# Second attention of a two-layer kernel: three rotating banks for transposes, another order of the steps of all engines, value products of three groups together, and the maximum subtracted in two places

## The reference, cut to what matters

```python
q = layernorm(x) @ w_q + b_q          # 128 x 256, 16 heads of 16
k = ctx @ w_k + b_k
v = ctx @ w_v + b_v
s = einsum('bhqd,bhkd->bhqk', q, k) / 4
p = softmax(s, axis=-1)
x = x + einsum('bhqk,bhkd->bhqd', p, v) @ w_o + b_o
```

## Time and profile before

| what | us |
|---|---|
| median of three runs | 687.03 (685.39 to 689.8) |
| the profiled execution, its own time | 685.72 |
| its span in the trace | 684.0 |
| busy in the span: TensorE matmuls | 545.5 |
| weight loads | 376.4 |
| VectorE | 404.1 |
| ScalarE | 296.6 |
| GpSimd | 170.5 |

### The profile page before, as it was taken

One profiled execution on the slowest core, in us unless ns is written; L12 is line 12 of the kernel. 1 busy time (PEld: TensorE's weight loads), 2 busy tenths in 40 slices (PEclk: granted clock), 3 DMA queues, 4 the chain that ended last, 5 costly groups with the idle time before them and its releaser, 6 DMA issues.

```text
span 684.0 us, 10069 instructions
## 1 busy us (share of the span) xinstructions
PE 545.5 (80%) x3430; PEld 376.4 (55%) x3430; DVE 404.1 (59%) x900; ACT 296.6 (43%) x582; POOL 170.5 (25%) x214
## 2 busy tenths in 40 slices
PE   0979998699899100996899999976149999999993
PEld 0658765344344000885676666646137777766772
DVE  6558789544499798675578887758733233211111
ACT  1436596143599695000477777752003112221210
POOL 4425441000000000002222222101035455456333
PEclk9989999799999655998699999998659999999997
DMA  8600000000000001500000000003102235554411
GB/s 266 206 0 2 1 0 2 0 0 1 0 0 0 0 0 49 197 0 1 0 2 32 2 32 2 33 1 124 35 21 97 84 120 167 176 165 134 153 54 39
DMA packets 30152, 37.57 MB, mean 55 GB/s; under 512 B 6560, under 2 KB 25888, under 8 KB 30112
## 3 DMA queue, kind: packets, MB, share of 16 engines
q1 hardware_dynamic: 27040, 29.07, 13.1%
q0 software_dynamic: 3072, 7.95, 3.8%
HBM read 30.14 MB, written 6.88 MB: 54 GB/s over the span
## 4 chain that ended last, share of the span: by engine, by line
PE 51%; DVE 18%; issue 11%; ACT 8%; DMA 6%; POOL 4%; DVEq 1%; another core or an unknown queue 0%; POOLq 0%; SPq 0%; ACTq 0%
PE pC L1390 6%; PE pA L1553 4%; DMA arena<-out,token 4%; PE pC L1427 4%; PE pB L1436 3%; PE pB L1563 3%; POOL arena L479 3%; PE pA L1421 3%; PE pB L1411 3%; PE pB L1496 2%; PE pC L1277 2%; PE pA L1351 2%; DVE arena L1011 2%; ACT arena L556 2%; PE pC L1351 2%
## 5 line engine op out<-in xcount | busy, mean ns | idle before, releaser
L453 POOL TENSOR_TENSOR arena<-KT,par 128x256 f32<-128x256 f32 x32 | 19.0, 614 | 235.2 <-PE pC L1390 210.5
L722 ACT ACTIVATE arena<-pA 128x320 f32<-128x320 f32 x64 | 27.9, 437 | 107.0 <-PE pA L1553 73.0
L1553 PE MATMUL pA<-arena 128*128 128x320 f32 x256 | 72.2, 440 | 0.9 <-ACT arena L722 0.9
L1179 DVE SCALAR_TENSOR_TENSOR arena<-pB,gcol,arena 128x256 f32<-128x256 f32 x16 | 7.1, 479 | 99.5 <-DMA arena<-out,token 96.7
L1553 PEld LDWEIGHTS pA<-arena 128*128 128x128 f32 x256 | 48.4, 192 | 23.1 <-issue 2.9
L1563 PE MATMUL pB<-arena 128*128 128x256 f32 x256 | 57.2, 381 | 3.4 <-DVE arena L1186 3.4
L1563 PEld LDWEIGHTS pB<-arena 128*128 128x128 f32 x256 | 48.1, 190 | 10.5 <-issue 4.0
L479 POOL DMA_INDIRECT arena<-token_rows,token x24 | 35.9, 1496 | 57.9 <-issue 37.4
L942 DVE TENSOR_REDUCE am<-arena (+1 forms) x48 | 32.0, 681 | 28.3 <-ACT arena L593 28.3
L1076 DVE TENSOR_REDUCE rm<-pA 128x16 f32<-128x2048 f32 x16 | 36.7, 2292 | 19.4 <-PE pA L1421 19.4
L1390 PE MATMUL pC<-wdnT,XIT 128*128 128x256 f32 x192 | 43.2, 389 | 2.4 <-DVE XIT L1031 2.4
(11 more groups left out here) (284 smaller groups left out, 1183.0 us busy)
## 6 DMA issues: line engine op xcount, KB each, us to landing
arena<-in_L_ffn_wi SPq DMA_DIRECT2D x8, 1024.0 KB, 8.5
arena<-in_L_ffn_wo SPq DMA_DIRECT2D x8, 1024.0 KB, 5.8
X<-in_x SPq DMA_DIRECT2D x4, 512.0 KB, 5.2
arena<-in_ctx SPq DMA_DIRECT2D x4, 512.0 KB, 5.8
out<-X SPq DMA_DIRECT2D x4, 512.0 KB, 2.9
token_rows<-arena SPq DMA_DIRECT2D x4, 512.0 KB, 3.0
arena<-in_L_ffn_w_up SPq DMA_DIRECT2D x1, 768.0 KB, 9.0
arena<-in_L_ffn_w_gate SPq DMA_DIRECT2D x1, 768.0 KB, 10.4
```

Of the source, the lines that this page charges most:

```text
L722: nc.scalar.activation(HT[:, u, f, :], ps[2 + f % 2][:, 0:ROWS], ACT.Relu).then_inc(s["h_relu"], 1)
L1553: last = mm(ps[2 + f % 2][:, 0:ROWS], WI[:, u, k, f * P:(f + 1) * P], XET[:, u, k, :], start=(k == 0), stop=(k == KD - 1))
```

## The change

It keeps the computation and the instructions of it, and changes where they write and in which order they stand:

- Three banks now rotate in place of two: `bank_q` and `bank_o` (the two of `pC`) and `bank_t` (`ps[4]`). `bank_q` holds c_turn, c_query and group 1; `bank_o` groups 0 and 3 and the output product; `bank_t` group 2, o_turn and a_turn.
- The groups are turned in the order 2, 0, 1, 3. The products of groups 2, 0 and 1 are one step, values_201; group 3's follow at the head of the next turn.
- The scores come at lag 0, late in the turn. less_max becomes less_first (lag 2, after add_attn) and less_last (lag 3, after attn_out and stats4). attn_out and add_attn are at lag 5, stats4 at 6, a_out at 4.
- On ScalarE exps_first is at lag 1 and late in the turn, exps_last first in the turn, and the four copies of the groups stand apart.
- The waits are those that the new order and banks need.

```diff
-        BANK_OF = (1, 1, 0, 1)
+        bank_q, bank_o, bank_t = pC[:, 0, :], pC[:, 1, :], ps[4]
+        bank_of = (bank_o, bank_q, bank_t, bank_o)
...
-            steps(act, NB, [(exps_first, 2), (os_copy, 3), (exps_last, 2), (xt_copy, 0), (pt_first, 2), (q_out, 0), (pt_second, 2), (at_copy, 3), (pt_rest, 2)])
+            steps(act, NB, [(exps_last, 2), (xt_copy, 0), (os_copy, 3), (pt_2, 2), (q_out, 0), (pt_0, 2), (exps_first, 1), (pt_1, 2), (pt_3, 2), (at_copy, 3)])
...
-            def less_max(b, u, h):
-                dve.wait_ge(s["rm_ready"], b + 1)
-                free_after(dve, s["pv_done"], b)
-                for e in range(2):
-                    part = slice(e * NH1 // 2, (e + 1) * NH1 // 2)
-                    V_.tensor_tensor(PR[:, u, part], sco[:, part], rm[:, u, part].unsqueeze(2).broadcast_to([P, NH1 // 2, P]), ALU.subtract).then_inc(s["s_sub"], 1)
-            steps(dve, NB, [(row_max, 2), (attn_out, 4), (less_max, 2), (norm3, 0), (add_attn, 4), (stats4, 5)])
+            def less_max(b, u, e):
+                part = slice(e * NH1 // 2, (e + 1) * NH1 // 2)
+                if not (isinstance(b, int) and b < 2):
+                    dve.wait_ge(s["pt_tr"], 4 * b - 5 + e)
+                V_.tensor_tensor(PR[:, u, part], sco[:, part], rm[:, u, part].unsqueeze(2).broadcast_to([P, NH1 // 2, P]), ALU.subtract).then_inc(s["s_sub"], 1)
+            def less_first(b, u, h):
+                dve.wait_ge(s["rm_ready"], b + 1)
+                less_max(b, u, 0)
+            def less_last(b, u, h):
+                less_max(b, u, 1)
+            steps(dve, NB, [(attn_out, 5), (stats4, 6), (less_last, 3), (norm3, 0), (row_max, 2), (add_attn, 5), (less_first, 2)])
...
             def c_turn(b, u, h):
                 pe.wait_ge(s["xn3"], b + 1)
-                if isinstance(b, int) and b < 4:
-                    if b >= 1:
-                        pe.wait_ge(s["qt_ready"], b)
-                else:
-                    pe.wait_ge(s["x3_ready"], b - 3)
+                if b >= 3:
+                    pe.wait_ge(s["pt_ready"], 4 * (b - 3) + 3)
+                elif b >= 1:
+                    pe.wait_ge(s["qt_ready"], b)
...
+            def turn_2(b, u, h):
+                pe.wait_ge(s["p_ready"], 2 * b + 2)
+                if b >= 2:
+                    pe.wait_ge(s["at_ready"], b - 1)
+                elif b == 1:
+                    pe.wait_ge(s["pt_ready"], 1)
+                turn_group(b, u, 2)
+            def turn_0(b, u, h):
+                pe.wait_ge(s["p_ready"], 2 * b + 1)
+                if b >= 2:
+                    pe.wait_ge(s["x3_ready"], b - 1)
+                elif b == 1:
+                    pe.wait_ge(s["pt_ready"], 4)
+                turn_group(b, u, 0)
+            def turn_1(b, u, h):
+                if b + 2 < NB:
+                    pe.wait_ge(s["qt_ready"], b + 3)
+                else:
+                    pe.wait_ge(s["pt_ready"], 4 * (b - 1) + 3)
+                turn_group(b, u, 1)
+            def turn_3(b, u, h):
+                pe.wait_ge(s["pt_ready"], 4 * b + 2)
+                turn_group(b, u, 3)
...
+            def values_201(b, u, h):
+                if b >= 1:
+                    pe.wait_ge(s["os_ready"], b)
+                value_group(b, u, 2, 1)
+                value_group(b, u, 0, 2)
+                value_group(b, u, 1, 3)
+            def values_3(b, u, h):
+                value_group(b, u, 3, 4).then_inc(s["pv_done"], 1)
             def o_turn(b, u, h):
                 pe.wait_ge(s["os_ready"], b + 1)
-                pe.wait_ge(s["pt_ready"], 4 * b + 3)
+                if b + 1 < NB:
+                    pe.wait_ge(s["pt_ready"], 4 * (b + 1) + 1)
+                else:
+                    pe.wait_ge(s["at_ready"], b)
...
             def a_turn(b, u, h):
                 pe.wait_ge(s["ao_ready"], b + 1)
-                if b + 3 >= NB:
-                    pe.wait_ge(s["x3_ready"], b)
-                else:
-                    pe.wait_ge(s["qt_ready"], b + 4)
...
             def a_out(b, u, h):
                 pe.wait_ge(s["at_ready"], b + 1)
+                if b + 1 < NB:
+                    pe.wait_ge(s["pt_ready"], 4 * (b + 1) + 4)
+                else:
+                    pe.wait_ge(s["x3_ready"], b)
...
-            flat(NB, [(scores1, 1), (o_turn, 3), (c_turn, 0), (turn_0, 2), (c_query, 0), (turn_1, 2), (values_0, 2), (a_turn, 3),
-                      (turn_2, 2), (values_1, 2), (turn_3, 2), (values_2, 2), (a_out, 3), (values_3, 2)])
+            flat(NB, [(values_3, 3), (c_turn, 0), (a_out, 4), (turn_2, 2), (c_query, 0), (turn_0, 2), (o_turn, 3), (turn_1, 2),
+                      (scores1, 0), (turn_3, 2), (a_turn, 3), (values_201, 2)])
```

More of the change, by code:

```diff
@@ L654, in xt_copy @@
                 free_after(act, s["c_q"], b)
-                nc.scalar.activation(XCT[:, u, 0:2], ps[4][:, 0:2 * P].rearrange("p (k n) -> p k n", k=2), ACT.Copy).then_inc(s["c_xt"], 1)
+                nc.scalar.activation(XCT[:, u, 0:2], bank_q[:, 0:2 * P].rearrange("p (k n) -> p k n", k=2), ACT.Copy).then_inc(s["c_xt"], 1)
             def q_out(b, u, h):
@@ L660, in q_out @@
                 for k in range(KD):
-                    last = nc.scalar.activation(QT[:, u, k, :], ps[4][:, (2 + k) * P:(3 + k) * P], ACT.Identity, scale=0.25, bias=bq[:, k:k + 1])
+                    last = nc.scalar.activation(QT[:, u, k, :], bank_q[:, (2 + k) * P:(3 + k) * P], ACT.Identity, scale=0.25, bias=bq[:, k:k + 1])
                 last.then_inc(s["qt_ready"], 1)
@@ L678, in os_copy, with pt_copy, pt_2, pt_0 @@
                 nc.scalar.activation(OS[:, u], ps[5][:, :].rearrange("p (t n) -> p t n", t=4), ACT.Copy).then_inc(s["os_ready"], 1)
[L680 to L684, removed]
+            def pt_copy(b, u, g, n):
+                act.wait_ge(s["pt_tr"], b * 4 + n)
+                nc.scalar.activation(PT[:, u, 4 * g:4 * g + 4, :], bank_of[g].rearrange("p (k n) -> p k n", k=4), ACT.Copy).then_inc(s["pt_ready"], 1)
+            def pt_2(b, u, h):
                 free_after(act, s["pv_done"], b)
[L686 to L693, removed]
+                pt_copy(b, u, 2, 1)
+            def pt_0(b, u, h):
+                pt_copy(b, u, 0, 2)
+            def pt_1(b, u, h):
+                pt_copy(b, u, 1, 3)
+            def pt_3(b, u, h):
+                pt_copy(b, u, 3, 4)
             def at_copy(b, u, h):
@@ L697, in at_copy @@
                 free_after(act, s["o_done"], b)
-                nc.scalar.activation(AT[:, u], ps[4][:, 0:2 * P].rearrange("p (k n) -> p k n", k=2), ACT.Copy).then_inc(s["at_ready"], 1)
-            steps(act, NB, [(exps_first, 2), (os_copy, 3), (exps_last, 2), (xt_copy, 0), (pt_first, 2), (q_out, 0), (pt_second, 2), (at_copy, 3), (pt_rest, 2)])
+                nc.scalar.activation(AT[:, u], bank_t[:, 0:2 * P].rearrange("p (k n) -> p k n", k=2), ACT.Copy).then_inc(s["at_ready"], 1)
+            steps(act, NB, [(exps_last, 2), (xt_copy, 0), (os_copy, 3), (pt_2, 2), (q_out, 0), (pt_0, 2), (exps_first, 1), (pt_1, 2), (pt_3, 2), (at_copy, 3)])
             rsqrt(4, NB)
@@ L1049, in add_attn @@
                 dve.wait_ge(s["bo_added"], b + 1)
-                V_.tensor_tensor(at(X, b), ps[4][:, 2 * P:4 * P], at(X, b), ALU.add).then_inc(s["x3_ready"], 1)
+                V_.tensor_tensor(at(X, b), bank_o[:, 0:D], at(X, b), ALU.add).then_inc(s["x3_ready"], 1)
             def stats4(b, u, h):
@@ L1061, in attn_out @@
                 dve.wait_ge(s["o_tr"], b + 1)
-                o = pC[:, 0, :].rearrange("p (h d) -> p h d", h=NH1)
+                o = bank_t.rearrange("p (h d) -> p h d", h=NH1)
                 V_.reciprocal(rs[:, u, :], o[:, :, DH1]).then_inc(s["rs_ready"], 1)
@@ L1397, in c_turn @@
                 pe.wait_ge(s["xn3"], b + 1)
-                if isinstance(b, int) and b < 4:
-                    if b >= 1:
-                        pe.wait_ge(s["qt_ready"], b)
-                else:
-                    pe.wait_ge(s["x3_ready"], b - 3)
+                if b >= 3:
+                    pe.wait_ge(s["pt_ready"], 4 * (b - 3) + 3)
+                elif b >= 1:
+                    pe.wait_ge(s["qt_ready"], b)
                 for k in range(KD):
-                    last = tr(ps[4][:, k * P:(k + 1) * P], T[:, u, k * P:(k + 1) * P], ident[:, :])
+                    last = tr(bank_q[:, k * P:(k + 1) * P], T[:, u, k * P:(k + 1) * P], ident[:, :])
                 last.then_inc(s["c_tr"], 1)
@@ L1410, in c_query @@
                     for k in range(KD):
-                        last = mm(ps[4][:, (2 + e) * P:(3 + e) * P], wT[0][:, k, e * P:(e + 1) * P], XCT[:, u, k, :], start=(k == 0), stop=(k == KD - 1))
+                        last = mm(bank_q[:, (2 + e) * P:(3 + e) * P], wT[0][:, k, e * P:(e + 1) * P], XCT[:, u, k, :], start=(k == 0), stop=(k == KD - 1))
                 last.then_inc(s["c_q"], 1)
@@ L1426, in turn_group, with value_group @@
                 for n in range(4):
```

(41 more changed lines are left out.)

## The result

The changed kernel takes 709.93 us (median of four runs, 709.36 to 710.94) against 688.4 of the kernel before (685.39 to 689.8): a ratio of 1.032, 95% interval 1.0279 to 1.0362. It is slower, as forecast, but by 21.5 us and not by 8.5, and it lies 1.9 us above the range. The profiled execution took 709.75 us, its span is 708.0.

The account below looks back on a forecast made before the run. TensorE bounded the old kernel (7.96 us a block), a TensorE-VectorE ring of 8.90 the new one. 12 x 0.94 = +11.3, fill -1.9, drain -0.9: +8.5, giving 695.5 us; own range 690 to 702, final range 685 to 708.

Parts of the forecast that it names:

- What bounds the kernel before: Second attention, middle block: TensorE sets the pace, busy 7.83 of 7.96 us.
- the ring: Within one turn of the changed kernel: o_turn, attn_out, stats4, less_last, scores, each waiting for the one before; chance 0.67.
- Prices on TensorE: Each TensorE step of a block priced in the new order; sum 6.82 us against 7.96.
- Length of the ring: Block period: TensorE's leg 6.46 us plus VectorE's leg behind o_turn 2.44, 8.90 in all; bounds 8.6 to 9.4.
- The cover of ScalarE: ScalarE's 6.14 us lie inside the block; its late exp before group 2's transposes might add 0 to 0.2 us.
- VectorE's own part: From scores' start through maximum, add and less_first: 4.90 us, then a wait of 1.5 us for o_turn.
- Fill: Stage's first blocks: second interval between row maxima shorter by 1.3 to 2.3 us, taken as 1.9; the others kept.
- Drain: Last maximum to last add, 18.0 us before: 0 to 1.8 us less, taken as 0.9.
- rival 3: TensorE's stands lower the clock; a quarter of the leg at half clock, +1.6 us a block, 705 to 720; chance 0.13.
- two clock rows: Earlier trace: clock fell with TensorE busy 0.79 of 3.00 us, stayed with 2.01 of 3.50; new kernel about 1.1 busy.
- Faster by shapes: Rival on TensorE's chain: fewer tile-shape changes, 7.96 to 6.82 us; VectorE then limits at 7.3 a block, 676; chance 0.12.
- The point of decision: TensorE's work from scores to o_turn, 6.46 us against VectorE's 4.90; below 5.5 the kernel would be faster.

Follow-up runs that it names:

- experiment 7: Changed kernel with less_last moved first in VectorE's list and add_attn moved behind less_first; 666.91 us, ratio 0.9733 to the kernel before.
- experiment 1: Changed kernel with only less_last moved first in VectorE's list, ahead of attn_out and stats4; 673.23 us, ratio 0.9795 to the kernel before.
- experiment 3: Changed kernel with stats4 moved behind less_last in VectorE's list, attn_out still ahead; 694.72 us, ratio 1.0109 to the kernel before.
- Experiment 6: Kernel before, with only the four value groups put together at the end of TensorE's turn; 676.88 us, ratio 0.9887.

## Why the prediction was right and wrong, point by point

- *What bounds the kernel before, and the ring*: right. Scores waited for less_last and less_last for attn_out, on the path that was named; opening it at one place gave some 36 us.
- *Prices on TensorE*: right, each to 0.05 us; that their sum was met to 0.01 in experiment 7 is luck. The one price without a row, 0.22 for a value group behind another, came out right: 1.01 for four, with 0.36 for the first.
- *Length of the ring*: 8.90 forecast, 8.82 measured. On TensorE c_turn cost 0.37 and not 0.41; behind o_turn the reciprocal starts after 0.03 us and not 0.07, and the other terms came out as listed, to 0.01. The cover of ScalarE held: no wait stands ahead of group 2's transposes at full clock, so nothing of the 0.2 kept for it was needed.
- *VectorE's own part*: the prediction had it through at 4.90 us and waiting 1.5 us for o_turn. It left out that the add waits for the output product, 0.74 us, so that only 0.65 is left at the reciprocal. Neither wait lasts beyond the end of o_turn, so the ring's length is not touched; but it is the add's wait that experiment 7 takes out of experiment 1.

```profile
360.22 0.42 DVE L1055 TENSOR_TENSOR X<-pC,X 128x256 f32<-128x256 f32 x1 [0.74 <-PE pC L1518]
362.43 0.26 DVE L1069 RECIPROCAL rs<-pB 128x16 f32<-128x16 f32 x1 [0.65 <-PE pB L1501]
```

- *Fill*: 1.9 us less forecast, 2.2 measured. *Drain*: 0.9 less forecast, 0.5 more measured, as the clock falls there too (at half from 468.4 to 471.8 us). In experiment 3, where the clock stays full there, it is 17.3 us, 1.2 less than before the change, within the 0 to 1.8 of the prediction.
- *The failed step*: rival 3, the clock, was taken as an alternative with a chance of 0.13 and its upper half was left out of the range, "It heals itself, ... so I take less than everything". It happened, on top of the forecast, and the sum had nothing for it; the runs show 14.5 us in the twelve intervals and one fall more in the drain, where the forecast was short by 13 us in all. The prediction's own sign, the clock leaving 1.00 between fill and end, appeared. Its price was nearly right: +1.6 a block were written down and 1.7 measured where the clock falls (10.52 less 8.82), though "a quarter of the leg" came from no row, and 3 of the 12 intervals have no fall. "In between", as the prediction said of its two clock rows, gave no ground for 0.13, and by its own price the time, 714, lay outside the range. The healing is real but lasts only until a later stand: the clock is at half in a block, full again in the same block, and the falls come back about every 10 us, once after 20.
- *Faster by shapes*: rightly rejected for this order, but the gain exists. Experiment 6 has 7.9 us on its own, and in experiment 7 the block is down to the whole sum of the new prices. The rule of the Trainium skill ("TensorEngine Tiling (Array Packing)", Key Properties: a change of mode drains the engine) speaks of that part rightly. The trace of the changed kernel has at full clock 0.17 to 0.33 us of idle before the loads behind such a change; the kernel lost more elsewhere than fewer changes gave. The point of decision (TensorE's leg against VectorE's) was the right one to compute. The prediction took 7.3 us as VectorE's own limit once the detour is gone; experiment 1 came at 7.1 to 7.2, which is near by accident: the 7.3 has attn_out and stats4 in the ring, which are out of it there, and has not the wait of 0.85 us ahead of the add. Experiment 7 showed that even this was an order of steps (the add ahead of less_first) and not VectorE's amount of work.

## What to carry to other kernels

With one set of buffers between two engines, write down the ring that fills and frees it, and look at everything that stands inside it in each engine's own list: a step that belongs to another block, placed there, lengthens the ring by all that this step waits for. Here the step that frees the scores goes first, and the reciprocal, the products, stats4 and norm3 fit into the time in which the scores are made (in experiment 7 they end before the maximum starts). And where a change makes TensorE stand for a fifth of a block that was full, price the clock as part of the forecast, not as an accident beside it.

## What the runs showed of the hardware that was not expected

The granted clock answered to idle time that is short against a block. With a stand of 1.92 to 2.01 us in each block of 8.8 it fell behind ten of twelve stands; with 1.6 to 1.7 of 8.5 once in the profile of one kernel (10.06 us interval), and with 1.55 to 1.64 never in another; with 1.05 to 1.14 of 8.8 never. Two stands of 0.9 us, with four transposes between them, let it fall six times, in the profile of a third. Each fall left it at half (1.2 GHz) for 3.4 us, and where that lay within one block it cost 1.5 to 1.9 us. A small step in the ring therefore has an effect beyond its size: stats4 was 0.33 us of it, and moving it took some 15 us off. In the twelve intervals it took 16.5, of which 4 are the ring (twelve times 0.33) and the rest the clock, and 1.7 more in the drain; 3.3 us came back outside the stage, which was not looked into.
